# Two of the six Q and K products of an attention block computed as halves of 64 rows

## Chip, cores and metric

The kernel runs on one core of one Trainium2 chip. The metric is the time of the program on the device in microseconds (us); smaller is better. Times of single runs are given as the median of three.

## What is computed

The reference is one attention layer over 128 graphs of 128 nodes, with a mask from an adjacency matrix, a residual and a layer normalisation (biases and the heads' reshaping are in the original as written here):

```python
q = heads(x @ Wq + bq); k = heads(x @ Wk + bk); v = heads(x @ Wv + bv)   # x: 128 x 128 x 384, 6 heads of 64
scores = einsum('bhqd,bhkd->bhqk', q, k) / sqrt(64)
probs = softmax(scores + where(adj, 0, -9e15)[:, None], axis=-1)
ctx = einsum('bhqk,bhkd->bhqd', probs, v)                                # back to 128 x 128 x 384
out = layernorm(x + ctx @ Wf + bf)
```

All arrays are float32. The kernel keeps the accuracy by splitting each operand of a large product into a rounded part (`_hi`) and the rest (`_lo`) and adding three products, hi x hi, hi x lo and lo x hi.

## The kernel before

The 128 batch elements are worked through in 32 groups of four (`GROUP`). One step handles one group on all five engines, each of which has its own queue in program order: TensorE (PE), VectorE (DVE), ScalarE (ACT), GpSimd (POOL) and SyncE (SP), which issues nearly all DMAs. Semaphores tie them together. `run_steps` runs steps 0 and 1 unrolled, then a loop of 14 turns of two steps (28 steps), then step 30 unrolled; the last group is handled by `ending`. Waits inside the loop are computed in registers.

In step g TensorE does, in this order (`step`, L528): the scores of group g (L425, 24 small products of 64 rows; the two heads of a pair lie on rows 0 to 63 and 64 to 127 and write different banks), three of the six Q and K products of group g+1 (`qk_product`, L456, nine matmuls of 128 rows and 512 columns each), the contexts of group g-1 (`ctx_product`, L429, pairs that write partitions 0 to 63 and 64 to 127), the other three Q and K products, the out products of group g-1 (`out_product`, L449) and the V products of group g+1 (`v_product`, L475).

PSUM has eight banks. Six form `scores_ps`; a step's score tiles fill them, `score_cols` (L170) says where: element 0 and the first two heads of element 1 lie in banks 0 and 3, the rest of element 1 and two thirds of element 2 in banks 1 and 4, the rest in banks 2 and 5. Contexts and out products later use banks 0, 3, 1 and 4 (`CTX_BANKS`). The other two banks are `work_ps`, through which Q, K and V products pass in turn.

VectorE masks the scores and finds row maxima (`mask_and_max`, L626, six instructions per element at L633, then a negation at L639), which frees the score banks (`max_found`). ScalarE does the exponentials (L825) and copies Q, K, V out of PSUM (`copy_qk`, L836; `copy_v`, L830). The probabilities are normalised by GpSimd (L979), turned in blocks by VectorE (`turn_blocks`, L642), stored to DRAM and loaded back in another order by SP (`store_blocks`, `load_blocks`), which makes them the contexts' operand. GpSimd also adds the bias to x (L962), makes the mask (L955) and normalises the output (L974). VectorE rounds off the rest: it turns x (`turn_x`), splits x and contexts into hi and lo (`split_x`, `split_ctx`), inverts the sums of the softmax (`invert_sums`), adds the residual (`add_residual`) and finds the statistics (`find_stats`).

The order on each engine is written out by hand in its `step`. A product waits before its first matmul for the operands and for the bank it will write; for the work banks this is the copy of the product two before (L463 to L466), for contexts it is `max_found` of the group whose scores lie there (L440).

## Time and profile before

| | |
|---|---|
| three runs, median | 1013.79 us (1013.69 to 1014.57) |
| the profiled execution | 1014.83 us, of which 1013.0 us lie between its first and last instruction (the span) |
| granted TensorE clock | 0.998 of full speed |
| busy share of the span | TensorE 99%, VectorE 70%, GpSimd 62%, ScalarE 58% |
| chain that ended last | TensorE 95%, ScalarE 2%, VectorE 1%, DMA 1% |
| DMA engines | 63.8% of their span busy with the main queue's packets, 175 GB/s |

Busy time counts an engine's own instructions, the span runs from the first to the last instruction, and matmuls overlap, so that their distance from start to start says more than their length.

### The profile page before, as it was taken

What the parts mean: (1) busy time and instruction counts of PE and PEld (TensorE: products, weight loads), DVE (VectorE), ACT (ScalarE), POOL (GpSimd) and SP (SyncE); (2) the same over time, 40 slices, a digit from 0 to 9 for tenths busy, and PEclk for the clock granted to TensorE, in tenths of its full rate; (3) what the DMA queues carried; (4) which work ended last, traced back from release to release, by engine and by line L of the source; (5) the groups of instructions that cost most, each with busy time, mean ns of one, the idle gap of its engine ahead of it and who ended that gap; (6) DMA issues with size and microseconds to landing.
All of it is one profiled execution on the core that took longest, in us unless ns stands there. A gap on an engine that the chain in (4) does not pass through costs nothing.

```text
span 1013.0 us, 26785 instructions
## 1 busy us (share of the span) xinstructions
PE 1001.5 (99%) x7156; PEld 901.5 (89%) x7156; DVE 705.5 (70%) x2829; ACT 583.8 (58%) x2121; POOL 629.8 (62%) x649
## 2 busy tenths in 40 slices
PE   9999999999999999999999999999999999999996
PEld 8888999888999889998899998899988999988986
DVE  4567766767667677667676676776676766767776
ACT  4665556664556655566645566554666455665552
POOL 2527755567665577555676655775556766557756
PEclk9999999999999999999999999999999999999999
DMA  7366676666766766766667667666676676675443
GB/s 207 81 182 182 185 191 189 174 185 174 197 170 181 187 168 175 195 169 182 181 174 196 168 184 187 163 180 187 171 189 177 176 191 176 181 183 157 150 150 130
DMA packets 339163, 178.06 MB, mean 176 GB/s; under 512 B 222529, under 2 KB 323009, under 8 KB 339137
## 3 DMA queue, kind: packets, MB, share of 16 engines
q1 hardware_dynamic: 337648, 176.77, 63.8%
q10 hardware_dynamic: 1488, 0.98, 0.3%
q8 instruction: 11, 0.18, 0.1%
q14 instruction: 16, 0.12, 0.0%
HBM read 102.96 MB, written 74.71 MB: 175 GB/s over the span
## 4 chain that ended last, share of the span: by engine, by line
PE 95%; ACT 2%; DVE 1%; DMA 1%; issue 0%; DVEq 0%; ACTq 0%
PE work_ps L408 20%; PE work_ps L409 19%; PE work_ps L410 19%; PE scores_ps L444 9%; PE scores_ps L425 9%; PE scores_ps L408 6%; PE scores_ps L409 6%; PE scores_ps L410 6%; ACT probs L825 1%; DMA y_sb<-in_L_gnn_Wq 1%; DVE stats L666 0%; DMA x_in<-in_x 0%; DVE probs L633 0%; ACT qT L843 0%; PE scores_ps L502 0%
## 5 line engine op out<-in xcount | busy, mean ns | idle before, releaser
L979 POOL TENSOR_TENSOR probs<-probs,inv_sum 128x768 f32<-128x768 f32 x128 | 188.5, 1473 | 332.4 <-DVE inv_sum L652 332.4
L825 ACT ACTIVATE probs<-probs,neg_max 128x128 f32<-128x128 f32 x768 | 298.9, 396 | 100.5 <-DVE neg_max L639 100.5
L633 DVE CUSTOM_DVE_ANT_0 probs<-scores_ps,mask_bias 128x128 f32<-128x128 f32 x768 | 172.0, 285 | 83.0 <-PE scores_ps L425 81.9
L974 POOL TENSOR_SCALAR y_sb<-y_sb,mean_var,rstd 128x384 f32<-128x384 f32 x120 | 198.8, 1656 | 21.5 <-POOL rstd L968 21.5
L834 ACT COPY v_sb<-work_ps 128x384 f32<-128x384 f32 x128 | 61.6, 481 | 215.4 <-PE work_ps L410 215.4
L825 ACT ACTIVATION_READ_ACCUMULATOR probs<-probs,neg_max 128x1 f32 x768 | 149.3, 194 | 0.0
L962 POOL TENSOR_TENSOR x_bias<-x_in,bias_row 128x384 f32<-128x384 f32 x128 | 127.6, 1019 | 9.0 <-DVE bias_row L788 9.0
L408 PE MATMUL scores_ps<-wf_hi,cT_hi 128*128 128x384 f32 x384 | 130.1, 339 | 0.0
L409 PE MATMUL scores_ps<-wf_lo,cT_hi 128*128 128x384 f32 x384 | 129.9, 338 | 0.0
L410 PE MATMUL scores_ps<-wf_hi,cT_lo 128*128 128x384 f32 x384 | 129.7, 338 | 0.0
L408 PE MATMUL work_ps<-wv_hi,xT_hi 128*128 128x384 f32 x381 | 128.1, 336 | 0.6 <-ACT qT L843 0.4
L410 PE MATMUL work_ps<-wv_hi,xT_lo 128*128 128x384 f32 x381 | 127.5, 335 | 0.0
L409 PE MATMUL work_ps<-wv_lo,xT_hi 128*128 128x384 f32 x381 | 127.4, 334 | 0.0
L645 DVE STREAM_TRANSPOSE p_turned<-probs 128x768 f32<-128x768 f32 x126 | 120.9, 960 | 5.3 <-DMA p_out<-p_turned 3.7
L408 PE MATMUL work_ps<-xT_hi,wq_hi 128*128 128x512 f32 x288 | 116.1, 403 | 0.1
L408 PE MATMUL work_ps<-xT_hi,wk_hi 128*128 128x512 f32 x288 | 115.8, 402 | 0.0
L409 PE MATMUL work_ps<-xT_lo,wq_hi 128*128 128x512 f32 x288 | 113.0, 392 | 0.0
L409 PE MATMUL work_ps<-xT_lo,wk_hi 128*128 128x512 f32 x288 | 112.5, 391 | 0.0
L410 PE MATMUL work_ps<-xT_hi,wq_lo 128*128 128x512 f32 x288 | 112.4, 390 | 0.0
L410 PE MATMUL work_ps<-xT_hi,wk_lo 128*128 128x512 f32 x288 | 112.1, 389 | 0.0
L843 ACT ACTIVATE kT<-work_ps,bk_col 128x512 f32<-128x512 f32 x96 | 65.2, 679 | 61.1 <-PE work_ps L410 61.1
L660 DVE TENSOR_TENSOR y_sb<-scores_ps,x_bias 128x384 f32<-128x384 f32 x120 | 65.4, 557 | 47.6 <-PE scores_ps L410 47.6
(78 smaller groups left out, 1886.9 us busy)
## 6 DMA issues: line engine op xcount, KB each, us to landing
p_out<-p_turned SPq DMA_DIRECT2D x126, 384.0 KB, 2.8
pT<-p_out SPq DMA_DIRECT2D x504, 96.0 KB, 2.3
x_in<-in_x SPq DMA_DIRECT2D x128, 192.0 KB, 3.0
x_blocks<-in_x SPq DMA_DIRECT2D x360, 64.0 KB, 2.4
out<-y_sb SPq DMA_DIRECT2D x120, 192.0 KB, 2.2
adj_u<-in_adj SPq DMA_DIRECT2D x32, 64.0 KB, 2.1
out<-xT SPq DMA_DIRECT2D x4, 192.0 KB, 1.9
out<-qT SPq DMA_DIRECT2D x4, 192.0 KB, 2.1
```

Source lines behind the costliest of these rows:

```text
L408: nc.tensor.matmul(dst, s_hi, m_hi, start=k == 0, stop=False)
L409: nc.tensor.matmul(dst, s_hi, m_lo, start=False, stop=False)
L410: last = nc.tensor.matmul(dst, s_lo, m_hi, start=False, stop=k == n_chunks - 1)
L425: last = nc.tensor.matmul(scores_ps[:, score_cols(e, h)], qT[rows, c, h // 2, tokens(e)], kT[rows, c, h // 2, tokens(e)], start=True, stop ...
L444: last = nc.tensor.matmul(dst[half:half + HEAD, h // 2 * SEQ:(h // 2 + 1) * SEQ], v_sb[:, c % TURN * GROUP + e, h * HEAD:(h + 1) * HEAD], ...
L633: last = nc.vector.tensor_tensor_reduce(out=probs[:, e, h, :], in0=scores_ps[:, score_cols(e, h)], in1=mask_bias[:, e, :], scale=SCALE, sc ...
L645: nc.vector.transpose(p_turned[:, e % 2, :, :, :].rearrange("p b h j -> p h b j"), probs[:, e, :, :].rearrange("p h (b k) -> p h b k", b=B ...
L660: nc.vector.tensor_tensor(y_slot(e, n), ctx_bank(e)[:, 0:HID], x_bias[:, c % TURN * GROUP + e, :], ALU.add).then_inc(y_added, 1)
L825: last = nc.scalar.activation(probs[:, e, h, :], probs[:, e, h, :], ACT.Exp, bias=neg_max[:, e, h:h + 1], scale=1.0, accum_out=row_sum[:, ...
L962: nc.gpsimd.tensor_tensor(x_bias[:, slot, :], x_in[:, slot, :], bias_row[:, :], ALU.add).then_inc(x_biased, 1)
L974: nc.gpsimd.tensor_scalar(y_slot(e, n), y_slot(e, n), mean_var[:, at, 0:1], rstd[:, at, 0:1], ALU.subtract, ALU.mult).then_inc(y_ready, 1)
L979: nc.gpsimd.tensor_tensor(probs[:, e, :, :], probs[:, e, :, :], inv_sum[:, e, :].unsqueeze(2).broadcast_to([P, HEADS, SEQ]), ALU.mult).the ...
```

## The change

Two of the six Q and K products of a step, the first of Q and the first of K, are computed as couples. Each matmul of 128 rows becomes two of 64 rows, one on the upper and one on the lower half of the array, which write two different PSUM banks. ScalarE copies the one half, with the bias, to qT or kT (`copy_half`), and VectorE adds the other half from PSUM to it (`sum_halves`). Q's halves go to the two work banks, K's to score banks 0 and 3 once masks 0 and 1 of the running group are done. These two products alone stand between scores and contexts; the other four follow the contexts. The contexts move to banks 1, 4, 2 and 5 (the old banks for the last two groups), wait for masks 2 and 3 accordingly, and the orders on VectorE and ScalarE are written anew. SP's and GpSimd's queues keep their order, and the products of the very first group stay whole.

```diff
+HALVED = 2
+HALF_BANKS = ((6, 7), (0, 3))
-CTX_BANKS = (0, 3, 1, 4)
+CTX_BANKS = (1, 4, 2, 5)
+LATE_CTX_BANKS = (0, 3, 1, 4)
...
+        def half_bank(j, half):
+            bank = HALF_BANKS[j][half]
+            return work_ps[bank - 6][:, :] if bank >= 6 else scores_ps[:, bank * BANK:(bank + 1) * BANK]
...
+        def copies(g, j):
+            return (NJ - HALVED) * g + j + 1
...
             def scores(i, c):
                 g, n = TURN * i + c, first_of(i, c)
-                past(pe, qk_copied, g, per=NJ)
+                pe.wait_ge(qk_copied, copies(g, NJ - 1))
+                if not isinstance(g, int) or g > 0:
+                    pe.wait_ge(qk_summed, HALVED * g)
...
             def ctx_product(i, c, e):
...
-                    past(pe, max_found, first_of(i, c) + GROUP + max(e, 1) - (e == 3))
-                dst = ctx_bank(e)
+                    masked = (1 if e < 2 else 2) if isinstance(g, int) and g == LAST - 1 else (2 if e < 2 else 3)
+                    past(pe, max_found, first_of(i, c) + GROUP + masked)
+                dst = ctx_bank(e, n)
...
             def qk_product(i, c, j):
...
-                if j < 2:
-                    past(pe, v_copied, max(n - GROUP, 0) + 2 + j if isinstance(n, int) else n - GROUP + 2 + j)
+                if isinstance(g, int) and g == 0:
...
+                elif j < HALVED + 2:
+                    pe.wait_ge(qk_summed, HALVED * (g - 1) + 1)
                 else:
-                    past(pe, qk_copied, g * NJ + j - 2)
+                    pe.wait_ge(qk_copied, copies(g, j - 2))
...
+            def qk_halves(i, c, j):
+                mat, m = QK_JOBS[j]
+                n, cols = first_of(i, c), slice(m * P, (m + 1) * P)
+                past(pe, xT_split, n + GROUP - 1)
+                if j == 0:
+                    past(pe, v_copied, n - 1)
+                else:
+                    past(pe, max_found, n - GROUP + j)
+                for k in range(KC):
+                    for w, moving in ((w_hi, xT_hi), (w_hi, xT_lo), (w_lo, xT_hi)):
+                        for half in range(2):
+                            rows = slice(half * HEAD, (half + 1) * HEAD)
+                            last = nc.tensor.matmul(half_bank(j, half), w[mat][rows, k, cols],
+                                                    moving[rows, c % TURN, k, :],
+                                                    start=k == 0 and w is w_hi and moving is xT_hi,
+                                                    stop=k == KC - 1 and w is w_lo)
+                last.then_inc(qk_done, 1)
...
             def step(i, c):                      # TensorE
                 scores(i, c)
-                for j in range(HALF):
-                    qk_product(i, c + 1, j)
+                for j in range(HALVED):
+                    qk_halves(i, c + 1, j)
                 if real(g - 1):
                     for e in range(GROUP):
                         ctx_product(i, c - 1, e)
-                for j in range(HALF, NJ):
+                for j in range(HALVED, NJ):
                     qk_product(i, c + 1, j)
...
+            def sum_halves(i, c, j):             # VectorE
+                mat, m = QK_JOBS[j]
+                dst = (qT if mat == "q" else kT)[:, c % TURN, m, :]
+                dve.wait_ge(half_copied, HALVED * (TURN * i + c - 1) + j + 1)
+                nc.vector.tensor_tensor(dst, half_bank(j, 1), dst, ALU.add).then_inc(qk_summed, 1)
...
                 mask_and_max(3, n + 3)           # VectorE, step, after masks 0 to 2 and invert_sums(0)
+                sum_halves(i, c + 1, 0)
+                invert_sums(1, n + 1)
+                sum_halves(i, c + 1, 1)
                 turn_x 0, 1
-                invert_sums(1); turn_x 2, 3; turn_blocks(0); split_ctx 0, 1; turn_blocks(1)
-                invert_sums(2); split_ctx 2, 3; turn_blocks(2); add_residual 0, 1; find_stats(0)
-                invert_sums(3); find_stats(1); add_residual 2, 3; turn_blocks(3); split_x 0 to 3; find_stats 2, 3
+                turn_blocks(0); invert_sums(2); turn_x 2, 3; turn_blocks(1); invert_sums(3); split_ctx 0, 1
+                turn_blocks(2); turn_blocks(3); split_ctx 2, 3; split_x(0); split_x(1); add_residual(0); find_stats(0)
+                split_x(2); add_residual(1); find_stats(1); split_x(3); add_residual(2); find_stats(2)
+                add_residual(3); find_stats(3)
...
+            def copy_half(i, c, j):              # ScalarE
...
+                past(act, qk_done, g * NJ + j)
+                past(act, scores_done, (g - 2) * GROUP + GROUP - 1)
+                nc.scalar.activation(dst[:, c % TURN, m, :], half_bank(j, 0), ACT.Identity,
+                                     bias=col[:, m:m + 1], scale=1.0).then_inc(half_copied, 1)
...
-                exps(0) with copy_qk 0 after two heads; copy_qk 1; exps(1); copy_qk 2; round_ctx 0, 1
-                exps(2) with copy_qk 3 after two heads; copy_qk 4; round_ctx 2, 3; exps(3); copy_qk 5
+                exps(0); copy_half 0; exps(1); copy_half 1; exps(2); exps(3) with copy_qk 2 after two heads
+                copy_qk 3; round_ctx 0, 1; copy_qk 4; round_ctx 2, 3; copy_qk 5
                 round_x 0 to 3; copy_v 0 to 3
```

The orders of VectorE and ScalarE at the end are shortened to the names of the calls.

## Rows read from the trace of the kernel before

**Rows 1.** The page's first part: busy us (share of the span) and instructions of each engine.
```profile
PE 1001.5 (99%) x7156; PEld 901.5 (89%) x7156; DVE 705.5 (70%) x2829; ACT 583.8 (58%) x2121; POOL 629.8 (62%) x649
```
**Rows 2.** One period of the loop: each engine's busy us, granted clock, DMA share, GB/s.
```profile
513.57:544.55 30.98, 30.98 (x224) 27.96 (x223) 21.90 (x89) 18.10 (x67) 19.84 (x20) 1.00 0.64 174
```
**Rows 3.** Timeline of TensorE around the scores: start us, us, engine, line, form, count.
```profile
516.31 0.49 PE L425 MATMUL scores_ps<-kT,qT 64*128 64x128 f32 x4
516.31 2.95 PE L425 MATMUL scores_ps<-kT,qT 64*128 64x128 f32 x48
519.19 0.50 PE L408 MATMUL work_ps<-xT_hi,wq_hi 128*128 128x512 f32 x1
519.53 0.40 PE L409 MATMUL work_ps<-xT_lo,wq_hi 128*128 128x512 f32 x1
519.77 0.40 PE L410 MATMUL work_ps<-xT_hi,wq_lo 128*128 128x512 f32 x1
```
**Rows 4.** The same timeline later in the step; twelve matmuls lie from the first to the second.
```profile
531.19 0.39 PE L408 MATMUL work_ps<-xT_hi,wk_hi 128*128 128x512 f32 x1
...
533.91 0.39 PE L408 MATMUL work_ps<-xT_hi,wq_hi 128*128 128x512 f32 x1
```
**Rows 5.** The timeline of TensorE at the beginning of the kernel, transposes before a product.
```profile
17.67 0.82 PE L502 MATMUL scores_ps<-ident,x_in 128*128 128x128 f32 x6
...
18.55 0.39 PE L409 MATMUL work_ps<-xT_lo,wq_hi 128*128 128x512 f32 x1
```
**Rows 6.** Timeline of VectorE in the same step of the loop: masks and negations.
```profile
519.64 0.36 DVE L639 TENSOR_SCALAR neg_max<-row_max 128x6 f32<-128x6 f32 x1
520.00 0.29 DVE L633 CUSTOM_DVE_ANT_0 probs<-scores_ps,mask_bias 128x128 f32<-128x128 f32 x1
...
521.27 0.08 DVE L633 DVE_READ_ACCUMULATOR2_ANT row_max<- 128x1 f32 x1
521.39 0.58 DVE L639 TENSOR_SCALAR neg_max<-row_max 128x6 f32<-128x6 f32 x1
521.88 0.28 DVE L633 CUSTOM_DVE_ANT_0 probs<-scores_ps,mask_bias 128x128 f32<-128x128 f32 x1
```
**Rows 7.** Timeline of ScalarE in that step; six exponentials lie between the last two.
```profile
520.03 0.40 ACT L825 ACTIVATE probs<-probs,neg_max 128x128 f32<-128x128 f32 x1 [3.14 <-DVE neg_max L639]
...
524.38 0.39 ACT L825 ACTIVATE probs<-probs,neg_max 128x128 f32<-128x128 f32 x1
...
526.69 0.67 ACT L843 ACTIVATE qT<-work_ps,bq_col 128x512 f32<-128x512 f32 x1
```
**Rows 8.** Timeline of VectorE in step 30, which is unrolled: the first negation and mask 1.
```profile
953.12 0.51 DVE L639 TENSOR_SCALAR neg_max<-row_max 128x6 f32<-128x6 f32 x1
953.34 0.29 DVE L633 CUSTOM_DVE_ANT_0 probs<-scores_ps,mask_bias 128x128 f32<-128x128 f32 x1
```
**Rows 9.** Timeline of GpSimd in the step of the loop: output normalisations, bias additions.
```profile
515.96 1.66 POOL L974 TENSOR_SCALAR y_sb<-y_sb,mean_var,rstd 128x384 f32<-128x384 f32 x1 [0.18 <-POOL rstd L968]
...
518.32 1.65 POOL L974 TENSOR_SCALAR y_sb<-y_sb,mean_var,rstd 128x384 f32<-128x384 f32 x1 [0.18 <-POOL rstd L968]
519.94 2.98 POOL L962 TENSOR_TENSOR x_bias<-x_in,bias_row 128x384 f32<-128x384 f32 x3
```
**Rows 10.** Timeline of VectorE in that step: two turns of x, a turned block.
```profile
525.77 1.04 DVE L617 STREAM_TRANSPOSE xT<-x_blocks 128x384 f32<-128x384 f32 x2
...
527.88 0.93 DVE L645 STREAM_TRANSPOSE p_turned<-probs 128x768 f32<-128x768 f32 x1
```
**Rows 11.** Timeline of SP's queue: first store of turned blocks, second block's first load.
```profile
528.85 0.33 SPq L316 DMA_DIRECT2D p_out<-p_turned  x1
...
536.36 1.85 SPq L325 DMA_DIRECT2D pT<-p_out  x4
```
**Rows 12.** Timeline of VectorE: from one output's statistics to its variance.
```profile
538.45 0.55 DVE L666 BATCH_NORM_STATS2 stats<-y_sb 128x6 f32<-128x384 f32 x1
...
539.41 0.15 DVE L673 TENSOR_SCALAR var_eps<-mean_var 128x1 f32<-128x1 f32 x1
```

More of the change, by code:

```diff
@@ L162, in score_cols, with ctx_bank @@
             return slice(first, first + SEQ)
-        def ctx_bank(e):
-            bank = CTX_BANKS[e]
+        def ctx_bank(e, n):
+            bank = LATE_CTX_BANKS[e] if isinstance(n, int) and n >= (LAST - 1) * GROUP else CTX_BANKS[e]
             return scores_ps[:, bank * BANK:(bank + 1) * BANK]
+        def half_bank(j, half):
+            bank = HALF_BANKS[j][half]
+            return work_ps[bank - 6][:, :] if bank >= 6 else scores_ps[:, bank * BANK:(bank + 1) * BANK]
         bias_bank = scores_ps[:, 5 * BANK:5 * BANK + HID]
@@ L251, in attention_block @@
         qk_copied = sem("qk_copied")
+        half_copied = sem("half_copied")
+        qk_summed = sem("qk_summed")
         masked_ready = sem("masked_ready")
@@ L469, in qk_product @@
                     xT_hi[:, c % TURN, k, :], xT_lo[:, c % TURN, k, :]), qk_done)
+            def qk_halves(i, c, j):
[4 more added lines that the diff above has]
+                    past(pe, v_copied, n - 1)
+                else:
+                    past(pe, max_found, n - GROUP + j)
[8 more added lines that the diff above has]
+                last.then_inc(qk_done, 1)
             def v_operands(c, e):
@@ L482, in v_product @@
                 elif not isinstance(g, int) or g > 0:
-                    past(pe, qk_copied, g * NJ + NJ - 2 + e)
+                    pe.wait_ge(qk_copied, copies(g, NJ - 2 + e))
                 split_product(work_ps[e % 2][:, 0:HID], v_operands(c, e), v_done)
@@ L705, in step @@
                         split_ctx(e, n - GROUP + e)
-                turn_blocks(i, c, 2, n + 2)
-                if real(g - 1):
-                    for e in (0, 1):
-                        add_residual(i, c - 1, e, n - GROUP + e)
-                    find_stats(0, n - GROUP)
-                invert_sums(3, n + 3)
-                if real(g - 1):
-                    find_stats(1, n - GROUP + 1)
-                    for e in (2, 3):
-                        add_residual(i, c - 1, e, n - GROUP + e)
-                turn_blocks(i, c, 3, n + 3)
-                if real(g + 2):
-                    for e in range(GROUP):
-                        split_x(c, e, n + 2 * GROUP + e)
-                if real(g - 1):
-                    for e in (2, 3):
-                        find_stats(e, n - GROUP + e)
+                for e in range(GROUP):
+                    if real(g + 2):
+                        split_x(c, e, n + 2 * GROUP + e)
+                    if real(g - 1) and e > 0:
+                        add_residual(i, c - 1, e - 1, n - GROUP + e - 1)
+                        find_stats(e - 1, n - GROUP + e - 1)
+                if real(g - 1):
+                    add_residual(i, c - 1, 3, n - GROUP + 3)
+                    find_stats(3, n - GROUP + 3)
             def ending():
@@ L817, in round_ctx @@
                 past(act, out_done, n - GROUP)
-                nc.scalar.copy(cT_hi[:, e, :, :], chunks(ctx_bank(e))).then_inc(cT_hi_ready, 1)
+                nc.scalar.copy(cT_hi[:, e, :, :], chunks(ctx_bank(e, n))).then_inc(cT_hi_ready, 1)
             def exps(e, n, first=0, end=HEADS):
@@ L848, in step @@
                 g, n = TURN * i + c, first_of(i, c)
-                exps(0, n, end=2)
-                copy_qk(i, c + 1, 0)
-                exps(0, n, first=2)
-                copy_qk(i, c + 1, 1)
-                exps(1, n + 1)
-                copy_qk(i, c + 1, 2)
-                if real(g - 1):
-                    for e in (0, 1):
-                        round_ctx(e, n - GROUP + e)
-                exps(2, n + 2, end=2)
-                copy_qk(i, c + 1, 3)
-                exps(2, n + 2, first=2)
-                copy_qk(i, c + 1, 4)
-                if real(g - 1):
-                    for e in (2, 3):
-                        round_ctx(e, n - GROUP + e)
-                exps(3, n + 3)
+                for e in range(HALVED):
+                    exps(e, n + e)
+                    copy_half(i, c + 1, e)
+                exps(2, n + 2)
+                exps(3, n + 3, end=2)
+                copy_qk(i, c + 1, 2)
+                exps(3, n + 3, first=2)
+                for half in range(2):
+                    copy_qk(i, c + 1, 3 + half)
+                    if real(g - 1):
+                        for e in (2 * half, 2 * half + 1):
+                            round_ctx(e, n - GROUP + e)
                 copy_qk(i, c + 1, 5)
```

25 lines of the change are left out of this document (16 added, 9 removed).

## The prediction

> **What bounds the kernel.** Read the page's first part first: TensorE's matmuls are busy for 99% of the span, the next engine for 70% [rows 1]. Then one period of the loop: in the 30.98 us between equal places of two steps TensorE is busy all of it, at full granted clock, while VectorE has 21.90 us of work, GpSimd 19.84 and ScalarE 18.10 [rows 2]. So a step is as long as TensorE's instruction stream, and time can be won in two ways only: fewer or shorter matmuls, or less lost where one kind of matmul follows another. It is lost as soon as TensorE waits for another engine; in the steady steps it never does now. All offsets below (+x) count from the first matmul of a step's scores, at 516.31 in the step shown [rows 3].
>
> **The change, first part: a change of array shape goes.** The scores use the array as two halves of 64 rows, the Q and K products all 128 rows, the contexts two halves of columns. The time of a shape change is read around the scores [rows 3]. Between the first two pairs of score matmuls and the whole block lie 22 pairs in 2.95 - 0.49 = 2.46 us, 0.112 us each; 24 pairs would take 2.69, and the block takes 2.88 (516.31 to 519.19). The 0.19 over is lost at the entry and the exit. The first product behind takes 0.34 (519.19 to 519.53), where one in the middle of a product takes 2.72 / 12 = 0.227 [rows 4]: 0.11 more, a weight load that could not run ahead. The entry holds such a load too, which leaves 0.08 of the 0.19 for the exit. So scores to products costs 0.08 + 0.11, about 0.20 (bounds: 0.11, the load alone, and 0.30, load and all of the 0.19). That it is the shape and not the number format is seen at the beginning of the kernel, where six transposes, of 128 rows too, lead into a product: 0.88 us from the first of them to the product's second matmul [rows 5], of which the product's first takes 0.227 and each transpose 0.109, with nothing left over. With the two products in the scores' shape this change goes once a step; the entry into the scores and both sides of the contexts stay. Removed: 31 steps (all but the last) x 0.20 = 6.2 us. Without any new wait the period would be 30.97 - 0.20 = 30.77.
>
> **Second part: the halves themselves.** Nine matmuls become 18 of 64 rows, that is nine pairs. A pair of scores passes 128 columns twice in 0.112; four times 128 columns once would be 0.224 by that. Full products take 0.227, and directly behind the scores, while VectorE reads the score banks, 0.24 (519.53 less 0.11, to the next). I take 0.227 a pair, as now, with 0.224 and 0.235 as bounds. The Trainium skill (TensorE: Matmul & The Clock Gate, section Measured speedup vs the span model) gives 3.07x for four row tiles, 77% of the ideal; at that share a pair would be an estimated 0.295. The scores speak against it: 0.112 for a pair beside 0.109 for one transpose of as many columns [rows 3, 5].
>
> **Third part: a new wait for mask 1.** The second pair of halves writes score banks 0 and 3, so it waits until VectorE has masked the first two elements (`max_found`). In the step shown the last instruction of mask 1 starts at 521.27 and lasts 0.08: +5.04 [rows 6]. From there to TensorE's first weight load I take 0.07: ScalarE starts 0.03 after the negation that frees it (519.64 + 0.36, then 520.03 [rows 6, 7]), and bounds are 0.03 and 0.10. The load can't run ahead of the wait, 0.11 as above. The halves of K would start to stream at +5.22. Without the wait they would start after 24 pairs and the first half-product: 0.11 + 2.69 + 9 x 0.227 = +4.84 (+4.92 with 0.235). TensorE therefore stands still for 0.30 to 0.38 us a step, and the saving of 0.20 is inside that: with the start of K's halves pinned to mask 1 it no longer matters how smoothly Q's follow the scores. Net of both: +0.10 to +0.18, I take +0.13. Queued behind this wait on TensorE is everything else of the step; the scores of the next step, and with them the masks, come later by as much.
>
> **Fourth part: the contexts now stand earlier and in other banks.** The third and fourth wait for all four masks. Mask 2 starts at +5.57 [rows 6]; it and mask 3 take 1.35 each (520.00 to 521.35) with two short instructions of some 0.2 each between: +8.7. TensorE gets there at 5.22 + 9 x 0.227 + 0.1, and half of a context block (48 matmuls of 128 columns like the scores, so an estimated 2.9 [rows 3]): +8.8. That is even; 0 to 0.1 a step, I take 0.02. Next margins: the first sum (behind mask 3, some 0.7 long, taken from the copy of the same size, 0.67 [rows 7]) ends at +9.6, and the third product, which needs it to free the work banks, comes at +10.2. The split of the third context sits behind the fourth turned block on VectorE. It is due after 36 matmuls of 0.227 and 18 of the out products (0.170, an estimate from 0.227 by 384 of 512 columns), less a load of 0.2 that runs ahead: +21.3; by the chain below it is done at +21.1. ScalarE issues the same copies as before, in another order, and VectorE's two sums (1.4 us) fit in its 9 us of idle time. These cost nothing, but the last cover is 0.2 us thick.
>
> **The sum.** 28 of the 31 steps run in the loop: 28 x (0.13 + 0.02) = +4.2 us. In the three unrolled steps mask 1 starts sooner behind mask 0 (0.22 after the negation's start, not 0.36 [rows 6, 8]), so wait and saving are about equal: 0. The profiled execution took 1014.83 us, 1.04 above the median of the runs shown: 1019.0 for it, **1018.0** for the median. Its own bounds: +0.04 a step (pairs of 0.224, a reaction of 0.03) gives 1015; +0.27 (pairs of 0.235, all of the contexts' wait) gives 1021.5.
>
> **Rival 1: GpSimd holds mask 1 back (slower still).** In the step shown the second negation lasts 0.58 and mask 2 starts only at 521.88, when the second of GpSimd's three bias additions ends (519.94 + 2 x 2.98 / 3 = 521.93) [rows 6, 9]. The first negation met only the end of a normalisation. The new order moves GpSimd. Roughly: six exps take 2.31 and a copy 0.6 [rows 7], so the second half-copy ends at +3.55 + 2 x 2.9 = +9.35, its sum at +10.1; two transposes of x and the first turned block (1.04 and 0.93 [rows 10]) end at +12.1; SP needs 7.51 from its first store to the first load behind the second (528.85 to 536.36 [rows 11]), and the fourth turned block waits for that store: +19.65 to +20.55; two splits of contexts, two of x and one residual, half a us each, +22.9; statistics 1.11 [rows 12], +24.0; four normalisations of 2.36 (515.96 to 518.32 [rows 9]), +33.5, which is +2.4 in the next step of 31.1. The bias additions then run from +2.4, +3.4 and +4.4. The first negation starts at +3.33, at the end of the first addition, and is free. Were GpSimd 0.1 to 0.5 us earlier, it would meet the second one and mask 1 would start up to 0.6 later than now; 0.5 us later, up to 0.3. With 0.3 to 0.6 in 28 steps: +8 to +17 on top, 1026 to 1035. For it: the margin is below what I can carry through; against it: stores that land late shift GpSimd to the harmless side.
>
> **Rival 2: the wait is shorter than the saving (faster).** In the loop the first negation lasts 0.36 and mask 1 starts as it ends [rows 6]. If the negation is what holds mask 1, then, with GpSimd elsewhere, mask 1 may start 0.22 after the negation's start, as in rows 8, and is through 0.14 sooner: a wait of 0.16 to 0.24, net 0.04 to -0.04 a step, 1012.5 to 1015. The contexts' wait goes by as much. With mask 1 early enough for no wait at all, 6.2 us go: 1007.6. The Trainium skill (SBUF — State Buffer, section SBUF: two separate sides) has VectorE block fully while GpSimd holds the pair of ports they share, which would make the negation the holder. Against it: in an unrolled step a negation of 0.51 did not keep the mask from starting 0.22 after it began [rows 8], so the 0.36 of the loop is more likely the loop's own.
>
> **Rival 3: the halves don't run side by side.** Then 18 more matmuls of 0.227, 4.1 us a step, +126 us: 1140. At the 0.295 of the skill's share the halves of Q end at +5.45, after mask 1, and the sum is 18 x 0.068 - 0.20 = +1.0 a step: 1045 (an estimate). Against both: the scores' pairs.
>
> **How the numbers follow.** Forecast 0.44 (1015 to 1021.5, a tenth of it below 1015.8), rival 1 0.21, rival 2 0.30 (half of it within 2 us of now, half 1007.6 to 1011.8), rival 3 0.05. The range leaves out rival 3, the far end of rival 1 and the far end of rival 2: 1009.5 to 1032. A measurement of this kernel can tell about 0.2% (2 us) from no change. Faster by more: half of rival 2, 0.15. Within: the other half and a tenth of the forecast, 0.19. Slower by more: the rest, 0.66.
>
> **What would show it.** Right: matmuls of the second half-product begin 0.3 to 0.4 us late in each loop step, at about +5.2, released by VectorE's masks; no lost load between scores and the first halves; a period of 31.1. Rival 1: bias additions over the first negation, mask 1 past +5.2, a period of 31.4 to 31.7. Rival 2: mask 1 through by +4.9. Rival 3: pairs far over 0.24. It would also be wrong if VectorE's tail or the second store came so late that the out products wait for split contexts.

## The result, and the profile after

The changed kernel takes 1034.79 us (median of four runs, 1032.35 to 1036.81), the kernel before 1013.76 beside it: 1.020 times as long (95% interval 1.0188 to 1.0212). Slower was forecast, but 1018.0 with 1009.5 to 1032.0; the time lies above the range. The profiled execution of after is the longest of the four, 1036.81 us, with a span of 1035.0. Line numbers (L507) are those of the kernel whose profile is quoted, and shift a little from one kernel to the next.

Where the 22.0 us between the two spans (1013.0 and 1035.0) lie is read from the starts of the score blocks on TensorE's timeline:

| | before | after | difference |
|---|---|---|---|
| up to the scores of step 4 | 144.63 | 154.84 | +10.2 |
| steps 4 to 29, mean of one | 30.973 | 31.428 | +0.455, 26 times: +11.8 |
| from the scores of step 30 to the end | 63.07 | 63.03 | 0 |

So there are two losses of nearly one size, and the one of the beginning was not in the sum at all.

Part 1 of the page, and one loop step (step 10) in the view by windows, as in rows 1 and 2:

```profile
PE 1008.8 (97%) x7714; PEld 899.2 (87%) x7714; DVE 754.4 (73%) x2891; ACT 585.2 (57%) x2121; POOL 630.9 (61%) x649
```
```profile
343.36:374.79 31.43, 31.12 (x243) 27.78 (x242) 23.50 (x90) 18.12 (x66) 19.83 (x21) 1.00 0.65 179
```

TensorE is no longer busy for the whole of a loop step. What it waits for is in the view of waits (engine, line, what released it: us in total, times, longest); PEld are its weight loads, and the last line is VectorE's:

```profile
PE scores_ps L507 <- DVE row_max L675: 8.4, 22, 0.5
PE scores_ps L423 <- DVE cT_lo L651: 4.9, 3, 3.0
...
PEld scores_ps L507 <- DVE row_max L675: 20.6, 28, 0.9
PEld scores_ps L462 <- DVE row_max L675: 8.6, 24, 0.4
PEld scores_ps L423 <- DVE cT_lo L651: 6.0, 4, 3.3
```
```profile
DVE p_turned L694 <- DMA p_out<-p_turned: 70.5, 32, 5.4
```

K's halves (L507) wait for the masks in each of the 28 loop steps. The out products (L423) wait for split contexts in three places only (their loads in four), but for up to 3 us. VectorE's turned blocks wait 70.5 us in all for their buffer to be stored, where they waited 3.7 before.

The loop step on TensorE, to be held against rows 3:

```profile
343.36 2.95 PE L442 MATMUL scores_ps<-kT,qT 64*128 64x128 f32 x48
346.06 0.48 PE L507 MATMUL work_ps<-xT_hi,wq_hi 64*128 64x512 f32 x2
346.37 0.39 PE L507 MATMUL work_ps<-xT_lo,wq_hi 64*128 64x512 f32 x2
...
347.99 0.40 PE L507 MATMUL work_ps<-xT_hi,wq_lo 64*128 64x512 f32 x2
348.70 0.50 PE L507 MATMUL scores_ps<-xT_hi,wk_hi 64*128 64x512 f32 x2 [0.31 <-DVE row_max L675]
```

Q's halves follow the scores 2.70 us after their start, where the product of before came 2.88 after; seven pairs from 346.37 take 1.62 us, 0.231 each. K's halves should follow at 348.22 (347.99 + 0.23) and come at 348.70. They wait for mask 1, and mask 1 is late. VectorE, from the end of mask 0 to the first instruction of mask 2, and GpSimd beside it:

```profile
346.57 0.08 DVE L675 DVE_READ_ACCUMULATOR2_ANT row_max<- 128x1 f32 x1
346.69 0.70 DVE L681 TENSOR_SCALAR neg_max<-row_max 128x6 f32<-128x6 f32 x1
347.30 0.28 DVE L675 CUSTOM_DVE_ANT_0 probs<-scores_ps,mask_bias 128x128 f32<-128x128 f32 x1
...
348.56 0.08 DVE L675 DVE_READ_ACCUMULATOR2_ANT row_max<- 128x1 f32 x1
348.68 0.65 DVE L681 TENSOR_SCALAR neg_max<-row_max 128x6 f32<-128x6 f32 x1
349.24 0.28 DVE L675 CUSTOM_DVE_ANT_0 probs<-scores_ps,mask_bias 128x128 f32<-128x128 f32 x1
```
```profile
346.35 2.95 POOL L1013 TENSOR_TENSOR x_bias<-x_in,bias_row 128x384 f32<-128x384 f32 x3
```

The three bias additions start at +2.99 from the step's first score, about 0.98 each: the first ends at 347.33, where mask 1 begins, and the third at 349.30, where mask 2 begins. The two negations between last 0.70 and 0.65 us; in rows 6 they were 0.36 and 0.58. So mask 1 ends at +5.28 (348.56 + 0.08), 0.24 later than in the kernel before, and mask 2 begins at +5.88 in place of +5.57.

Half of what the beginning loses, 5.3 us, is lost in step 1 (scores at 52.53). SP's queue, VectorE and TensorE there, and two windows of it:

```profile
70.54 3.17 SPq L340 DMA_DIRECT2D pT<-p_out  x4
73.75 0.43 SPq L331 DMA_DIRECT2D p_out<-p_turned  x1
```
```profile
77.01 0.98 DVE L694 STREAM_TRANSPOSE p_turned<-probs 128x768 f32<-128x768 f32 x1 [5.41 <-DMA p_out<-p_turned]
77.92 0.98 DVE L651 TENSOR_TENSOR cT_lo<-scores_ps,cT_hi 128x384 fp32r<-128x384 f32 x2
```
```profile
75.17 0.34 PE L425 MATMUL scores_ps<-wf_hi,cT_lo 128*128 128x384 f32 x1
78.49 0.44 PE L423 MATMUL scores_ps<-wf_hi,cT_hi 128*128 128x384 f32 x1 [2.98 <-DVE cT_lo L651]
...
80.08 0.52 PE L423 MATMUL scores_ps<-wf_hi,cT_hi 128*128 128x384 f32 x1
...
82.00 0.52 PE L423 MATMUL scores_ps<-wf_hi,cT_hi 128*128 128x384 f32 x1
```
```profile
75.35:78.40 3.05, 0.16 (x1) 0.00 (x0) 1.39 (x3) 0.00 (x0) 0.00 (x0) 1.00 0.82 171
...
80.00:82.40 2.40, 2.40 (x9) 2.40 (x9) 2.19 (x7) 0.00 (x0) 0.80 (x1) 0.50 0.36 142
```

The chain reads downwards: the second store is issued at 73.75, 21.2 us into the step. The fourth turned block waits 5.41 us for it. The splits of contexts 2 and 3 stand behind that block, and the third out product waits 2.98 us for the first of them. Soon after TensorE goes on, the granted clock falls from 1.00 to 0.50, from 2.4 to 1.2 GHz: from 80.08 to 82.00 lie six matmuls, 0.32 apart, where they are 0.18 apart in the first two out products. The four out products take 11.1 us in place of 6.3.

The store is no later than it was. In the kernel before it was issued at +21.3 in step 1 (scores at 50.91), and the fourth turned block came at +26.1:

```profile
72.25 0.43 SPq L316 DMA_DIRECT2D p_out<-p_turned  x1
```
```profile
77.02 0.97 DVE L645 STREAM_TRANSPOSE p_turned<-probs 128x768 f32<-128x768 f32 x1
```

There the splits stood ahead of that block; the change put them behind it.

### The profile page after: what moved, and what is told of

The parts are those of the page before. It is cut to its first block, busy times and chain, and to the rows that moved or that the text cites. A ratio compares the mean times of both kernels' runs of the same rounds, so it can differ in the third digit from the quotient of the medians.

```text
span 1035.0 us, 28006 instructions
## 1 busy us (share of the span) xinstructions
PE 1008.8 (97%) x7714; PEld 899.2 (87%) x7714; DVE 754.4 (73%) x2891; ACT 585.2 (57%) x2121; POOL 630.9 (61%) x649
## 4 chain that ended last, share of the span: by engine, by line
PE 81%; DVE 10%; issue 3%; ACT 2%; DMA 2%; DVEq 1%; SPq 0%; ACTq 0%
PE work_ps L423 15%; PE work_ps L425 14%; PE work_ps L424 14%; PE scores_ps L462 8%; DVE probs L675 8%; PE scores_ps L423 6%; PE scores_ps L424 6%; PE scores_ps L425 6%; PE scores_ps L507 6%; PE scores_ps L442 5%; DMA p_out<-p_turned 2%; ACT probs L871 2%; SPq L340 0%; DVEq L73 0%; DVE row_max L675 0%
## 5 line engine op out<-in xcount | busy, mean ns | idle before, releaser
L1019 POOL TENSOR_TENSOR rstd<-var_eps,minus_half 128x1 f32<-128x1 f32 x128 | 80.2, 628 | 235.7 <-DVE var_eps L722 235.7
L694 DVE STREAM_TRANSPOSE p_turned<-probs 128x768 f32<-128x768 f32 x126 | 120.4, 956 | 70.5 <-DMA p_out<-p_turned 70.5
L871 ACT ACTIVATION_READ_ACCUMULATOR probs<-probs,neg_max 128x1 f32 x768 | 155.1, 202 | 0.0
L423 PE MATMUL scores_ps<-wf_hi,cT_hi 128*128 128x384 f32 x384 | 131.2, 342 | 4.9 <-DVE cT_lo L651 4.9
L423 PE MATMUL work_ps<-wv_hi,xT_hi 128*128 128x384 f32 x381 | 127.9, 336 | 0.0
L462 PEld LDWEIGHTS scores_ps<-pT,v_sb 128*64 128x64 f32 x1536 | 82.7, 137 | 16.0 <-DVE row_max L675 8.6
L442 PEld LDWEIGHTS scores_ps<-kT,qT 64*128 64x128 f32 x1536 | 88.2, 188 | 8.5 <-issue 7.7
L462 PE MATMUL scores_ps<-pT,v_sb 128*64 128x128 f32 x1536 | 93.0, 276 | 2.2 <-issue 2.0
L442 PE MATMUL scores_ps<-kT,qT 64*128 64x128 f32 x1536 | 94.4, 276 | 0.1
L423 PE MATMUL work_ps<-xT_hi,wq_hi 128*128 128x512 f32 x195 | 79.7, 409 | 1.7 <-DVE qT L689 1.7
L651 DVE TENSOR_TENSOR cT_lo<-scores_ps,cT_hi 128x384 fp32r<-128x384 f32 x128 | 64.6, 543 | 23.0 <-ACT cT_hi L864 22.6
L423 PEld LDWEIGHTS scores_ps<-wf_hi,cT_hi 128*128 128x128 f32 x384 | 72.5, 189 | 7.3 <-DVE cT_lo L651 6.0
```

Source lines behind the costliest of these rows:

```text
L423: nc.tensor.matmul(dst, s_hi, m_hi, start=k == 0, stop=False)
L442: last = nc.tensor.matmul(scores_ps[:, score_cols(e, h)], qT[rows, c, h // 2, tokens(e)], kT[rows, c, h // 2, tokens(e)], start=True, stop ...
L462: last = nc.tensor.matmul(dst[half:half + HEAD, h // 2 * SEQ:(h // 2 + 1) * SEQ], v_sb[:, c % TURN * GROUP + e, h * HEAD:(h + 1) * HEAD], ...
L694: nc.vector.transpose(p_turned[:, e % 2, :, :, :].rearrange("p b h j -> p h b j"), probs[:, e, :, :].rearrange("p h (b k) -> p h b k", b=B ...
L871: last = nc.scalar.activation(probs[:, e, h, :], probs[:, e, h, :], ACT.Exp, bias=neg_max[:, e, h:h + 1], scale=1.0, accum_out=row_sum[:, ...
L1019: nc.gpsimd.tensor_tensor(rstd[:, at, :], var_eps[:, at, :], minus_half[:, :], ALU.pow).then_inc(rstd_ready, 1)
```

## The experiments

Two losses, so two theories, each with an edit that removes its cause alone. **Theory G**: GpSimd's additions hold the negations and so the masks, in each loop step. **Theory D**: the fourth turned block, waiting for a store, holds the splits, in the first steps. Beside them stands **theory A**: VectorE's masks bind the step, and whatever TensorE saves in front of them is waited away. Its rivals are that the wait in front of K's halves is the loss by itself, and that the halves cost more than whole products.

The runs stand in the order of the argument; 9 ran beside 1 to 3, and 8 last. A mean step is the time between the scores of step 4 and of step 30, divided by 26. Each ratio is to the kernel before run beside it (medians 1013.8 to 1014.1).

| kernel | scores of step 4 at | mean step, 4 to 29 | time, median | ratio to before, 95% |
|---|---|---|---|---|
| before | 144.63 | 30.973 | 1013.8 | |
| after | 154.84 | 31.428 | 1034.8 | 1.0188 to 1.0212 |
| 1: earlier release | 151.98 | 31.365 | 1032.5 | 1.0170 to 1.0204 |
| 2: additions moved | 152.44 | 31.137 | 1026.3 | 1.0106 to 1.0140 |
| 3: splits moved | 147.00 | 31.337 | 1026.0 | 1.0104 to 1.0138 |
| 4: both moves | 146.37 | 31.125 | 1020.5 | 1.0050 to 1.0081 |
| 5: all three | 146.47 | 31.025 | 1016.6 | 1.0011 to 1.0030 |
| 6: five, and mask 3 ahead | 146.41 | 30.753 | 1009.2 | 0.9932 to 0.9960 |
| 7: six, whole products | 145.65 | 30.973 | 1015.6 | 1.0004 to 1.0022 |
| 8: five, whole products | 146.48 | 31.015 | 1016.8 | 1.0018 to 1.0038 |
| 9: after, whole products | 148.74 | 31.344 | 1028.8 | 1.0128 to 1.0162 |

**1. K's halves released earlier.** The banks 0 and 3 that they write are free after the second head of element 1's mask; the change waits for all six.

```diff
+                    if e == 1 and h == 1:
+                        last.then_inc(banks_free, 1)
...
-                    past(pe, max_found, n - GROUP + j)
+                    past(pe, banks_free, TURN * i + c - 1)
```

> The second pair of halves (K) is released when VectorE has masked the first two heads of element 1 (banks 0 and 3 hold no more), not when mask 1 is through; nothing else is changed. Theory A (VectorE's chain of masks as a whole binds the step: the contexts behind the halves need masks 2 and 3): K's halves start without a wait at about +4.85, but the wait reappears in front of the third context, which comes no sooner than mask 3, about +9.0; the period stays within 0.1 us of 31.45 and the time between 1032 and 1036. Rival B (the wait in front of K's halves is the loss by itself): the 0.4 to 0.8 us of each step come back, 1015 to 1024.

Measured: 1032.5 us. TensorE's timeline of step 10 (scores at 340.40):

```profile
345.26 0.40 PE L508 MATMUL scores_ps<-xT_hi,wk_hi 64*128 64x512 f32 x2
...
347.69 1.53 PE L463 MATMUL scores_ps<-pT,v_sb 128*64 128x128 f32 x24 [0.22 <-DVE row_max L676]
```

K's halves now follow Q's without a gap, and the same masks stop the contexts instead. The step is 0.06 shorter, and the time is at the low end of what theory A expected. This wait alone is not the loss; what matters is when the masks end.

**2. GpSimd's additions moved** behind its normalisation of the probabilities, where VectorE makes no negations.

```diff
-                for e in range(3):
-                    add_bias(i, c, e, n + e)
                 normalise_probs(0, n)
...
-                add_bias(i, c, 3, n + 3)
...
                 for e in (2, 3):
                     normalise_probs(e, n + e)
+                for e in range(GROUP):
+                    add_bias(i, c, e, n + e)
```

> GpSimd's four bias additions are moved behind the last normalisation of probabilities, where it has been idle for some 8 us; the operations are the same. Theory G (the additions lie over the first two negations and hold mask 1 and mask 2 back): the first two negations last 0.17 to 0.4, mask 1 starts at +3.69 in every loop step, mask 3 ends at about +8.5 where it ended at +9.0, the period falls from 31.45 to about 31.1, the time by 8 to 10 us to 1025. Rival (the masks are late for a reason of VectorE's own): no change, 1033 to 1037.

Measured: 1026.3 us, and steps of 31.137. VectorE after mask 0 and after mask 1, GpSimd, and TensorE's first pair of K's halves, all in step 10 (scores at 339.23):

```profile
342.56 0.17 DVE L681 TENSOR_SCALAR neg_max<-row_max 128x6 f32<-128x6 f32 x1
342.92 0.29 DVE L675 CUSTOM_DVE_ANT_0 probs<-scores_ps,mask_bias 128x128 f32<-128x128 f32 x1 [0.19 <-issue]
...
344.31 0.17 DVE L681 TENSOR_SCALAR neg_max<-row_max 128x6 f32<-128x6 f32 x1
```
```profile
340.42 1.65 POOL L1025 TENSOR_SCALAR y_sb<-y_sb,mean_var,rstd 128x384 f32<-128x384 f32 x1 [0.18 <-POOL rstd L1019]
...
355.69 3.95 POOL L1013 TENSOR_TENSOR x_bias<-x_in,bias_row 128x384 f32<-128x384 f32 x4
```
```profile
343.86 0.40 PE L507 MATMUL work_ps<-xT_hi,wq_lo 64*128 64x512 f32 x2
344.33 0.50 PE L507 MATMUL scores_ps<-xT_hi,wk_hi 64*128 64x512 f32 x2
344.67 0.40 PE L507 MATMUL scores_ps<-xT_lo,wk_hi 64*128 64x512 f32 x2
```

Without additions beside it a negation takes 0.17 us, mask 1 begins at +3.69 in place of +3.94, and every step is alike. Theory G holds for the loop. Mask 1 still begins 0.36 after the negation's start, as in the kernel before, though the negation itself takes only 0.17: so there it was not the negation that held mask 1. What is left of the wait of K's halves is 0.24 (344.33 against 343.86 + 0.23) and 0.11 for the load that can't run ahead (0.34 to the next pair in place of 0.23). The beginning is as bad as before: step 4 starts at 152.4.

**3. The splits moved** ahead of the fourth turned block.

```diff
                 turn_blocks(i, c, 2, n + 2)
-                turn_blocks(i, c, 3, n + 3)
                 if real(g - 1):
                     for e in (2, 3):
                         split_ctx(e, n - GROUP + e)
+                turn_blocks(i, c, 3, n + 3)
```

> VectorE splits contexts 2 and 3 before the fourth turned block, as the kernel before did, not behind it. Theory D (at the beginning the fourth turned block waits for a late store and holds the splits and with them the out products): the out products of steps 1, 2 and 3 take 6.34 us again where they took 11.1, 7.5 and 7.6, 7.2 us in all; later steps keep their period; 1027 to 1029. Rival (those steps are late because of SP's queue or the sums): the stall moves to another wait in the same steps, 1033 to 1037.

Measured: 1026.0 us. VectorE in step 1, and the window of its four out products:

```profile
70.70 0.98 DVE L651 TENSOR_TENSOR cT_lo<-scores_ps,cT_hi 128x384 fp32r<-128x384 f32 x2
75.08 0.98 DVE L694 STREAM_TRANSPOSE p_turned<-probs 128x768 f32<-128x768 f32 x1 [3.40 <-DMA p_out<-p_turned]
```
```profile
71.34:77.68 6.34, 6.34 (x37) 6.33 (x36) 2.91 (x6) 2.33 (x5) 0.00 (x0) 1.00 0.77 190
```

The block still waits 3.40 us for the store, but nothing that TensorE needs stands behind it: 6.34 us, busy throughout, clock 1.00. Theory D holds: step 4 starts 7.8 us sooner than in the first profile of after, 5.5 sooner than in the second (run 9). The time is a us under what was expected, for the loop, which was to stay as it was, gains 0.09 a step as well, since VectorE's tail ends sooner and GpSimd's additions with it: they run from +2.03, and then it is the second that holds mask 1.

**4. Both moves together**, to see whether they are two losses or one.

> Both moves at once: GpSimd's four bias additions behind its four normalisations, and the splits of contexts 2 and 3 ahead of the fourth turned block. If the two losses are separate (one a toll on every step of the loop, by GpSimd's additions over the masks; one a delay of steps 1 to 3, by the fourth turned block over the splits), they add up: the start of step 4 near 147 us as with the splits alone (154.8 in the changed kernel), steps of 31.13 to 31.15 as with the additions alone, together 1019 to 1022. What is then left above the kernel before is the wait of K's halves for mask 1 (0.16 a step, 4 to 5 us), step 0 (1.1) and step 1. If the two moves remove the same loss, the time stays at 1025 to 1026.

Measured: 1020.5 us, with the beginning of run 3 and the loop of run 2. They are two losses. The single moves gained 8.5 and 8.8, the two 14.3; most of the 3.0 between lies in the loop, where the moves gain 0.29 and 0.09 a step singly but 0.30 together (2.1 us in 26 steps): what run 3 gains through GpSimd can't be had twice.

**5. Both moves and the earlier release.**

> As the run with both moves, and K's halves wait for the second head of element 1's mask in place of the whole of it. Theory A (the wait of K's halves hides the saved shape change): without it K's halves follow Q's with no gap, the contexts start at +7.00 us as they do in the free steps of the run with the early release alone; the third context then waits for mask 3 (8.50 + 0.06), 0.2 behind where it could start, so a step is 30.95 to 31.0 and the time 1015 to 1017. If the halves themselves, and not the wait, cost the time, the step stays at 31.13 and the time at 1019 to 1022.

Measured: 1016.6 us, within the range, and steps of 31.025, just above theirs. VectorE's masks now stop the contexts, as the waits of TensorE's loads show, 56 times, two in each loop step:

```profile
PEld scores_ps L463 <- DVE row_max L676: 17.4, 56, 0.4
```

A step is 0.05 longer than in the kernel before, although the change of shape is gone. Step 0 became longer, 25.25 us in place of 23.73: there K's halves end sooner, and TensorE waits for the first sum, which stands behind mask 3. The windows of that wait and of what follows:

```profile
35.20:37.36 2.16, 0.26 (x3) 0.03 (x1) 2.08 (x13) 2.16 (x11) 1.93 (x3) 1.00 0.00 0
37.36:39.86 2.50, 2.50 (x6) 1.93 (x7) 2.18 (x4) 2.50 (x13) 2.00 (x3) 0.55 0.03 7
```

The clock is at 1.00 in the wait and at a mean of 0.55 behind it, near the lower level.

**6. Mask 3 ahead of the negation and the reciprocal that stood before it**, and in step 0 the first sum ahead of mask 3.

```diff
-                for e in range(3):
-                    mask_and_max(e, n + e)
-                invert_sums(0, n)
-                mask_and_max(3, n + 3)
-                sum_halves(i, c + 1, 0)
+                for e in range(3):
+                    mask_and_max(e, n + e, negated=e < 2)
+                if first:
+                    sum_halves(i, c + 1, 0)
+                mask_and_max(3, n + 3, negated=False)
+                for e in (2, 3):
+                    negate(e, n + e)
+                invert_sums(0, n)
+                if not first:
+                    sum_halves(i, c + 1, 0)
```

> As the run before, and on VectorE mask 3 comes ahead of the negation and the reciprocal that stood before it (it should end at +8.3 in place of +8.5), and in step 0 the first sum of halves stands ahead of mask 3. Theory A: with mask 3 out of the way the saving of 0.20 us a step shows for the first time: steps of 30.75 to 30.82, and step 0 shorter by about 1; 1008 to 1011, faster than the kernel before. If something later in the step takes the place of the waits (the out products for the split contexts, V's products, the next scores), the step stays at 30.95 or above and the time at 1014 or above.

Measured: 1009.2 us, 0.9946 of the kernel before (0.9932 to 0.9960). This is a version that beats both kernels, with the halves as the change has them. The gain over run 5 is the loop's, 0.27 a step: step 0 came down from 25.25 to 23.72 us, but step 1 went up from 30.75 to 32.48, and step 4 starts where it did.

**7. The same with whole products in place of the halves**, which brings back the change of shape and leaves the second bank unwritten.

```diff
-                        for half in range(2):
-                            rows = slice(half * HEAD, (half + 1) * HEAD)
-                            last = nc.tensor.matmul(half_bank(j, half), w[mat][rows, k, cols],
-                                                    moving[rows, c % TURN, k, :],
+                        last = nc.tensor.matmul(half_bank(j, 0), w[mat][:, k, cols],
+                                                moving[:, c % TURN, k, :],
```

> As the run before, with whole products in the places of the halves: nine matmuls on all 128 rows into the first of the two banks; the second bank is left unwritten, so two of the six pieces of Q and K are not what they should be, and everything else is done as before. This measures the shape change by itself where no wait hides it: theory A expects 0.18 to 0.22 us a step over 31 steps, 5.5 to 7 us more than the run before (1014 to 1018). If pairs of half products cost no less than one whole product and the change of shape is paid elsewhere, the two runs are equal within 1 us; the run with whole products on the changed kernel was 6 us faster than it, which speaks for that rival.

Measured: 1015.6 us, 6.4 more. TensorE at the end of the scores and one step by windows, first with the halves (scores at 330.93), then whole (scores at 331.49):

```profile
333.63 0.48 PE L508 MATMUL work_ps<-xT_hi,wq_hi 64*128 64x512 f32 x2
333.94 0.39 PE L508 MATMUL work_ps<-xT_lo,wq_hi 64*128 64x512 f32 x2
```
```profile
330.93:361.68 30.75, 30.75 (x242) 27.98 (x241) 22.43 (x90) 18.06 (x66) 19.70 (x21) 1.00 0.66 180
```
```profile
334.37 0.50 PE L506 MATMUL work_ps<-xT_hi,wq_hi 128*128 128x512 f32 x1
334.71 0.40 PE L506 MATMUL work_ps<-xT_lo,wq_hi 128*128 128x512 f32 x1
```
```profile
331.49:362.46 30.97, 30.97 (x223) 27.95 (x222) 22.55 (x90) 18.08 (x66) 19.37 (x20) 1.00 0.64 176
```

The first product starts 2.70 or 2.88 us after the scores and its second matmul 0.31 or 0.34 later: 0.21 a step of the 0.22 between the periods. The Trainium skill (TensorEngine Tiling (Array Packing), section Key Properties) says that switching the tiling mode drains TensorE; the trace fits that, with 0.18 us before the new shape starts, though it shows the time and not the drain itself.

**8. Run 5 with whole products**, where mask 3 still stands in the way.

> The run with the early release and both moves, with whole products in the places of the halves (the second bank unwritten, as before). There mask 3 held the third context to 31.03 us a step. If that wait hides the change of shape, whole products cost almost nothing here: contexts start at +7.22 in place of +7.00, the third still follows mask 3, steps of 31.02 to 31.1, and a time within 2 us of the run with halves (1016.6). If the change of shape is paid in full, 31.24 a step and 1022 to 1024.

Measured: 1016.8 us against 1016.6, steps of 31.015 against 31.025. The same change of shape that is worth 6.4 us between runs 6 and 7 is worth nothing here: the masks pin the contexts, and all that is saved in front of them is waited away.

**9. The changed kernel with whole products.**

> The two products are computed by nine matmuls of 128 rows into the first of their two banks instead of 18 of 64 rows; all waits, copies and sums stay as they are (the second bank isn't written by the products, so the sum adds what lies there). Theory A: the shape change behind the scores comes back and costs 0.20 us, but in front of the wait for the masks, which hides it: a period within 0.05 us of 31.45, 1032 to 1037. Rival (the saving arrives, only other losses are larger): 31 x 0.20 = 6 us more, 1041.

Measured: 1028.8 us, 6 less than the changed kernel, which neither theory expected. The loop is no dearer without the saving, as theory A says, though at 31.344 it is 0.08 below after's 31.428, and further from 31.45 than the 0.05 expected. The rest is the beginning: in step 1 its out products take 7.35 us in place of 11.1. To see how much of that is the same in each execution, the changed kernel and this one were each profiled once more.

> The changed kernel as it is, for a second profile: how much of its beginning is the same in every execution? In the first one the second store of turned blocks of step 1 was issued at +21.21 us, the fourth turned block waited 5.41 us for the one before it to be stored, TensorE stood 2.98 us before the third out product, its granted clock then fell to 0.50, and step 4 began at 154.8 us. If the stall belongs to the order of the work, this run has it too, between 2 and 3 us long and with the clock down behind it, and step 4 begins between 150 and 156; if it was one late transfer, step 4 begins before 150 and the clock stays at 1.00. The steps of the loop take 31.35 to 31.5 us in either case.

> The changed kernel with whole products in the places of the halves (nine matmuls on all 128 rows into the first bank, the second left unwritten) a second time. It was 6 us faster than the changed kernel, though a whole product brings the change of shape back. If that came from the beginning alone (a stall of 1.07 us before the third out product of step 1, and the clock at 1.00 behind it), this run shows a stall of TensorE under 2 us there, the clock at 1.00, and step 4 before 150 us. If the halves themselves cost time, its loop is shorter: under 31.2 us a step.

Measured: 1033.0 and 1029.3 us, the scores of step 4 at 152.47 and 147.91, mean steps of 31.380 and 31.367. The out products of step 1 in run 9, in its second profile, and in the second profile of the changed kernel, with the third one there:

```profile
71.91:79.26 7.35, 6.61 (x37) 6.28 (x36) 4.57 (x11) 2.33 (x5) 0.31 (x1) 1.00 0.78 217
```
```profile
71.06:78.32 7.26, 6.63 (x38) 6.30 (x36) 4.58 (x11) 2.33 (x5) 0.33 (x1) 1.00 0.82 223
```
```profile
77.19 0.44 PE L423 MATMUL scores_ps<-wf_hi,cT_hi 128*128 128x384 f32 x1 [1.73 <-DVE cT_lo L651]
```
```profile
72.11:80.46 8.35, 6.62 (x38) 6.29 (x36) 4.58 (x11) 2.33 (x5) 0.32 (x1) 1.00 0.75 207
```

The kernel with whole products came out as expected the second time. In the changed kernel the stall is there again, and step 4 starts within the 150 to 156 expected; but the stall is 1.73 us long, and the clock stays at 1.00, so that neither expectation fits whole. The stall's length follows one store: in these four profiles and those of runs 1 and 2 the third out product starts 4.2 to 4.7 us after the store is issued. The lower clock came behind the longer stall only. Together that makes 2.8 us in the out products of step 1 between two executions of one program.

The store follows the four loads issued in front of it: these took 3.17 us on SP's queue in the first profile of after and 2.40 in the second, 1.74 in both of whole products. The halves alone don't explain it: in run 5, which has them, the four took 1.73, in runs 1 to 4 and 6 from 2.46 to 2.87. The difference between after and run 9 is settled in its place (mainly the beginning, not the loop), not in its cause.

## Why the prediction was wrong

**What held.** The change of shape as a sum: 0.20 was read from rows 3 to 5, and runs 6 and 7 measure 0.22 a step. Its parts were wrong, and that they added up is luck: 0.08 was given to the scores' exit and 0.11 to a load that could not run ahead, but the exit costs 0.18, and of the load only 0.03 is saved. The first pair of halves still takes 0.31 where the others take 0.23, so the sign "no lost load between scores and the first halves" did not appear. The pairs of halves: 0.227 was taken, Q's take 0.231. The Trainium skill (TensorE: Matmul & The Clock Gate, section Measured speedup vs the span model) gives 3.07x for four row tiles. At that share of the ideal, 77%, a pair would be an estimated 0.295; that is not what two halves of 64 rows cost here. The wait for mask 1: TensorE was to lose 0.30 to 0.38, and run 2 shows 0.24 + 0.11; with the contexts' wait the net was to be +0.15 a step, and run 4 has 31.125 - 30.973 = +0.15. The forecast of 1018.0 is thus near the time of run 4, 1020.5, the change without its two other losses; of what lies between, 1.7 us are run 4's beginning, 1.0 of them step 0.

**Step that failed: GpSimd's place, and with it mask 1 at +5.04.** The third part took the end of mask 1 from the kernel before, +5.04; in after it is +5.28, because GpSimd's additions came to lie over the negations. That was rival 1, which put the additions at +2.4, where the first negation "starts at +3.33, at the end of the first addition, and is free". They started at +2.99. Two terms of that chain were short by about half a us each: the first output's statistics were to end at +24.0 and ended at +24.6 in step 10 (the fourth turned block began at +20.2, not +19.65), and from there to the additions of the next step it took 9.8 us, not four times 2.36. The text had the price for this side ("0.5 us later, up to 0.3"), and 0.3 is what a step lost: 31.428 - 31.125, 7.9 us in 26 steps. But it gave the rival 0.21, after writing that the margin was below what it could carry through; and it counted late stores as a shift "to the harmless side", when late by 0.6 is the side that pays. In all three places that the additions take in these profiles at the start of a step (+3.63 before, +2.99 after, +2.03 in run 3) they hold a negation: free is the narrow case.

**Step that failed: the fourth part's cover, read from one loop step.** "These cost nothing, but the last cover is 0.2 us thick" compared a split due at +21.3 with one done at +21.1. In after's step 10 that was close: the split began at +21.1, the third out product at +21.9, and TensorE did not wait. But the sum then put the unrolled steps at "0". In step 1 the fourth turned block began at +24.5, held by the store, and in steps 2 and 3 at +21.3 and +21.8; steps 1 to 3 lost 5.3, 1.4 and 1.9 us. Step 0 lost 1.15: there are no contexts between K's halves and the third product, so the wait for the first sum, for which the text found a margin in the loop, is bare. With 0.5 in front of step 0, that is the 10.2. The last sentence of the prediction names this very case ("the second store came so late that the out products wait for split contexts"), without a price or a chance. A cover of 0.2 us on a transfer's landing needed both, and the rows of before for step 1 were there to be read: the store that rows 11 imply, issued at +17.25 in the loop step (533.56), came at +21.3 in step 1.

**The range.** Its upper end was cut inside rival 1. The two losses can come together (run 4 shows that they are separate), and that case was not weighed at all: 1018.0, 7.9 for the loop and the 8.5 by which step 4 starts later in after than in run 4 make some 1034.

**Rival 2** is out as it was told: with GpSimd elsewhere, in run 2, mask 1 began 0.36 after the negation's start and not 0.22, as the text's own argument against the rival had it. But it named the prize: no wait at mask 1 was worth 1007.6 there, and run 6, which gets rid of the waits by the order of the work, took 1009.2. **Rival 3** is out: the halves run side by side, a pair in 0.23.

## What to carry to other kernels

A saving on the engine that bounds a kernel is worth nothing as long as a wait behind it is pinned to another engine: free the wait first, as runs 6, 7 and 8 show with 6.4 us or none for the same edit. When an edit moves one engine's work by half a us, look at what the other engines do at the new time, not only at whether the work fits. Price the first steps by rows of the first steps, and give any cover that is thinner than a transfer's scatter a chance of its own.

## What was not expected of the hardware

- A bias addition of GpSimd's (two operands in SBUF) holds VectorE's negation until it ends, 0.70 us in place of 0.17, and the mask queued behind the negation with it. The masks themselves run beside the additions at 0.28 us, as without them. The Trainium skill (SBUF — State Buffer, section SBUF: two separate sides) has one of the two engines block fully, for certain kinds of VectorE's operations only; the trace agrees, down to the mask's start at the addition's end.
- Behind a wait of 2.98 us TensorE's granted clock fell to 0.50, and the 18 matmuls of the third and fourth out product took 4.8 us; at 0.176 each they take 3.2. The stall cost half as much again as its length. Behind a wait of 2.21 us in run 2 the clock fell too (0.56 from 78.61 to 80.61); behind one of 1.73 at the same place, in the second profile of after, it stayed at 1.00.
- Taking a negation and a reciprocal from between masks 2 and 3 brought mask 3's end from +8.5 to +8.07, 0.44 us in place of the 0.2 expected: with nothing between them, mask 3 follows mask 2 without a gap.
- The issue of four loads on SP's queue took between 1.74 and 3.17 us at one and the same place of two kernels that differ only in TensorE's instructions. The cause is open.
